# Two stacked self-attention layers: the shift's small operations on GpSimd, and a third native slot in the last stage

## The reference

```python
q = einsum('rc,bcn->brn', Wq, xf) + bq     # 16 rows
k = einsum('rc,bcn->brn', Wk, xf) + bk     # 16 rows
v = einsum('oc,bcn->bon', Wv, xf) + bv     # 128 rows
attn = softmax(einsum('bri,brj->bij', q, k), axis=2)   # 1024 x 1024 per image
out = einsum('bcj,bij->bci', v, attn)
x = gamma * out + x
```

## Time and profile before

| | us |
|---|---|
| median of 3 runs | 213.25 (212.74 to 218.13) |
| the profiled execution | 212.72 |
| its span, first to last instruction | 210.9 |
| PE busy | 187.4 |
| DVE busy | 168.8 |
| ACT busy | 153.3 |
| POOL busy | 149.1 |

### The profile page before, as it was taken

One profiled execution on the slowest core, in us unless ns is written; L12 is line 12 of the kernel. 1 busy time (PEld: TensorE's weight loads), 2 busy tenths in 40 slices (PEclk: granted clock), 3 DMA queues, 4 the chain that ended last, 5 costly groups with the idle time before them and its releaser, 6 DMA issues.

```text
span 210.9 us, 3123 instructions
## 1 busy us (share of the span) xinstructions
PE 187.4 (89%) x1107; PEld 121.6 (58%) x1109; DVE 168.8 (80%) x162; ACT 153.3 (73%) x219; POOL 149.1 (71%) x95
## 2 busy tenths in 40 slices
...
GB/s 166 364 17 177 22 103 2 0 3 3 51 50 2 6 0 99 3 3 0 101 3 3 0 78 26 0 3 53 99 50 0 33 23 50 3 5 14 86 49 51
DMA packets 3871, 9.49 MB, mean 45 GB/s; under 512 B 545, under 2 KB 913, under 8 KB 3857
## 3 DMA queue, kind: packets, MB, share of 16 engines
...
HBM read 2.89 MB, written 2.10 MB: 24 GB/s over the span
## 4 chain that ended last, share of the span: by engine, by line
PE 61%; DVE 21%; ACT 7%; issue 4%; POOL 3%; DMA 2%; SPq 0%; DVEq 0%; POOLq 0%
PE out_psum L692 25%; PE out_psum L690 5%; PE ring L667 5%; PE ring L619 5%; PE ring L643 5%; ACT ring L433 5%; DVE shift_parts L542 5%; PE ring L629 5%; DVE attn_lo L519 5%; DVE shift L539 4%; PE out_psum L693 3%; PE out_psum L726 3%; DVE shift_parts L544 3%; DVE x_all L567 2%; DVE neg_max L524 2%
## 5 line engine op out<-in xcount | busy, mean ns | idle before, releaser
L524 DVE TENSOR_REDUCE neg_max<-ring 128x1 f32<-128x1024 f32 x64 | 76.1, 1220 | 17.5 <-PE ring L645 17.1
L433 ACT ACTIVATE ring<-ring,neg_max 128x1024 f32<-128x1024 f32 x64 | 69.6, 1087 | 19.6 <-DVE neg_max L524 19.5
L346 POOL TENSOR_TENSOR attn_lo<-attn,attn_hi 128x1024 fp32r<-128x1024 f32 x34 | 81.9, 2418 | 2.6 <-ACT attn_hi L451 1.8
L445 ACT ACTIVATE attn<-ring 128x1024 f32<-128x1024 f32 x64 | 63.7, 1025 | 15.5 <-PE ring L669 13.1
L341 POOL TENSOR_SCALAR attn_hi<-attn 128x1024 fp32r<-128x1024 f32 x35 | 39.1, 1124 | 39.8 <-ACT attn L445 36.0
L643 PE MATMUL ring<-qk_swapped,qk 64*128 64x512 f32 x56 | 26.6, 481 | 3.0 <-ACT ring L433 2.4
L669 PE MATMUL ring<-qk_swapped,qk 64*128 64x512 f32 x64 | 28.0, 467 | 0.0
L667 PE MATMUL ring<-qk,qk_swapped 64*128 64x512 f32 x64 | 27.6, 461 | 0.3 <-DVE shift_rows L553 0.2
L645 PE MATMUL ring<-qk,qk_swapped 64*128 64x512 f32 x56 | 27.0, 488 | 0.0
L693 PE MATMUL out_psum<-attn,v 64*128 64x512 f32 x56 | 26.4, 591 | 0.0
L692 PE MATMUL out_psum<-attn,v 64*128 64x512 f32 x56 | 26.4, 591 | 0.0
...
## 6 DMA issues: line engine op xcount, KB each, us to landing
...
qk<-shift_rows SPq DMA_DIRECT2D x7, 8.0 KB
```

The lines of the kernel that those rows point to most:

```text
L346: nc.gpsimd.tensor_tensor(attn_lo[:, k - 1], attn[:, k], attn_hi[:, k - 1].bitcast(fp32), ALU.subtract).then_inc(cut_made["lo", "gpsimd"], 1)
L433: nc.scalar.activation(e[:], e[:], ACT.Exp, bias=neg_max[s][:, i:i + 1], accum_out=row_sum[s][:, i:i + 1]).then_inc(sum_made, 1)
L445: nc.scalar.activation(attn[:, k], ring_tile("ET", s, k)[:].rearrange("p (a n) -> p a n", a=2), ACT.Exp).then_inc(attn_made, 1)
L524: nc.vector.tensor_reduce(neg_max[s][:, i:i + 1], ring_tile("E", s, i)[:], axis=AX.X, op=ALU.max, negate=True).then_inc(max_made, 1)
```

## The change

The three small operations of `parts` move from DVE to POOL: `cut_shift` is removed and `split_shift` does the same on POOL, where the copy is written as a multiplication by 1 plus 0. The parts of the second half of stage 0 lie in columns 8 to 15 of their tile, not in 0 to 7 (`parts_of`). In stage 7 slot 4 becomes native. The five orders are new. Counted over them: DVE has 9 `parts` and 4 `lo` fewer and one `v_lo` more (130 entries become 118); POOL has 9 `parts`, 3 `lo` and one `v_hi` more, one `hi` and one `v_lo` fewer (84 become 95); ACT has one `v_hi` fewer, PE one `PH` fewer. The matmuls of `warm` entries fall from 14 to 12. SP has the same 24 entries.

```diff
-NATIVES = [(0, 1, 4, 7), (0, 7), (0, 7), (0, 7), (0, 7), (0, 7), (0, 7), (0, 7)]
+NATIVES = [(0, 1, 4, 7), (0, 7), (0, 7), (0, 7), (0, 7), (0, 7), (0, 7), (0, 4, 7)]
...
@@ PE_ORDER: begin, around the shifts of stages 0 and 1, and the last stage
-raw.0.0.0 raw.0.1.1 QK.1.0.2 E.0.7.0 E.0.3.1 V.0.0.2 E.0.5.0 E.0.4.1 E.0.0.2 warm.0.4 E.0.2.0 E.0.1.1 E.1.6.2
-warm.0.4 E.0.6.0 warm.0.1 QK.2.0.1 shift.0.0.2 warm.0.3 ET.0.2.2 ET.0.1.0 warm.0.2 E.1.2.2 ET.0.0.1 shift.0.1.0
...
-E.2.5.1 V.1.0.2 ET.0.6.0 shift.1.1.1 PV.0.2 E.2.2.2 ET.0.5.0 QK.3.0.1 E.2.4.0 ET.0.7.2 PV.0.4 ET.1.1.2 PH.0.6
...
-ET.7.2.1 ET.7.5.2 ET.7.6.0 PH.6.3 PH.6.5 PV.6.4 ET.7.4.1 ET.7.7.2 PH.6.6 PV.6.3 PV.6.6 PV.6.5 PV.6.1 ET.7.0.0
-ET.7.1.1 ET.7.3.2 PH.7.6 PH.7.5 PH.7.4 PH.7.2 PV.7.7 PV.7.6 PV.7.5 PV.7.4 PH.7.1 PH.7.3 PV.7.2 PV.7.1 PV.7.3 PV.7.0
+raw.0.0.0 raw.0.1.1 E.0.7.2 E.0.6.0 QK.1.0.1 E.0.2.2 E.0.3.0 E.0.4.1 warm.0.4 E.0.5.2 E.0.1.0 E.0.0.1 warm.0.2
+V.0.0.2 shift.0.1.0 warm.0.1 E.1.3.1 QK.2.0.0 shift.0.0.2 warm.0.3 ET.0.5.2 ET.0.2.1 warm.0.1 ET.0.3.2 E.1.7.0
...
+PV.0.1 E.2.2.2 V.1.0.0 shift.1.1.1 PV.0.3 ET.0.7.2 PV.0.2 E.2.7.1 ET.0.6.0 QK.3.0.2 ET.1.1.0 ET.1.2.1 PH.0.6 PH.0.5
...
+PV.5.7 E.7.3.2 ET.6.7.1 PV.5.6 PV.5.5 V.7.0.0 PH.6.3 PH.6.4 ET.6.2.2 ET.6.5.1 ET.6.0.0 PV.6.7 shift.7.1.1 PV.6.4
+PH.6.6 PH.6.1 PV.6.6 PH.6.5 PV.6.3 ET.7.6.0 ET.7.7.1 ET.7.3.2 PV.6.1 PV.6.5 PV.6.0 PH.6.2 ET.7.5.2 ET.7.1.0 ET.7.4.1
+PV.6.2 PH.7.6 ET.7.2.2 ET.7.0.1 PH.7.5 PV.7.6 PH.7.3 PV.7.7 PV.7.4 PV.7.5 PH.7.1 PH.7.2 PV.7.3 PV.7.1 PV.7.2 PV.7.0
...
@@ POOL_ORDER, whole
-mask.1.0 stack.1.0 v_lo.0.0 hi.0.2 lo.0.2 hi.0.3 lo.0.3 hi.0.6 lo.0.6 hi.0.5 v_lo.1.0 lo.0.5 hi.1.1 lo.1.1 hi.1.2
-lo.1.2 lo.1.3 hi.1.5 hi.1.6 hi.1.4 lo.1.5 hi.2.3 lo.1.6 lo.1.4 hi.2.1 v_lo.2.0 lo.2.3 hi.2.2 lo.2.2 hi.2.4 lo.2.5
-v_hi.3.0 lo.2.4 hi.3.2 hi.2.6 lo.2.6 hi.3.3 v_lo.3.0 lo.3.2 lo.3.3 v_hi.4.0 hi.3.4 lo.3.1 v_lo.4.0 hi.3.6 lo.3.6
-hi.4.2 lo.3.4 lo.4.1 lo.4.2 lo.4.3 hi.4.5 v_hi.5.0 hi.4.4 v_lo.5.0 hi.4.6 lo.4.4 lo.4.6 hi.5.2 hi.5.3 lo.5.3 hi.5.1
-lo.5.1 hi.5.5 lo.5.2 lo.5.5 hi.5.4 hi.5.6 lo.5.4 hi.6.3 v_hi.6.0 v_lo.6.0 hi.6.2 hi.6.4 lo.6.2 v_hi.7.0 lo.6.4
-lo.6.5 v_lo.7.0 hi.7.6 hi.7.4 lo.7.5 hi.7.1 hi.7.3
+mask.1.0 stack.1.0 parts.0.1 parts.0.0 v_lo.0.0 hi.0.2 hi.0.3 hi.0.5 lo.0.3 lo.0.5 parts.1.1 lo.0.2 v_hi.1.0 hi.0.6
+lo.0.6 hi.1.2 hi.1.1 hi.1.3 v_lo.1.0 lo.1.1 lo.1.2 v_hi.2.0 lo.1.3 parts.2.1 hi.1.4 hi.1.6 lo.1.4 hi.1.5 lo.1.6
+lo.1.5 hi.2.1 v_lo.2.0 hi.2.4 parts.3.1 hi.2.3 hi.2.2 lo.2.3 lo.2.2 lo.2.6 v_hi.3.0 lo.2.4 hi.2.5 lo.2.5 v_lo.3.0
+hi.3.2 hi.3.3 parts.4.1 lo.3.3 lo.3.1 lo.3.2 v_hi.4.0 hi.3.4 hi.3.6 lo.3.6 lo.3.4 v_lo.4.0 hi.4.3 lo.4.3 parts.5.1
+hi.4.1 lo.4.1 hi.4.5 v_hi.5.0 v_lo.5.0 lo.4.2 hi.5.3 lo.4.5 lo.4.6 hi.5.1 hi.5.2 parts.6.1 lo.5.2 lo.5.3 lo.5.1
+hi.5.5 hi.5.6 lo.5.4 lo.5.6 hi.6.3 hi.6.4 v_lo.6.0 lo.6.3 hi.6.6 lo.6.1 parts.7.1 lo.6.6 hi.6.2 lo.6.2 v_hi.7.0
+hi.7.6 hi.7.5 lo.7.5 hi.7.1 lo.7.3 lo.7.2
...
@@ SP_ORDER, begin
-swap.1.0 swap.0.0 swap.2.0 place.0.1 place.1.1 swap.3.0 place.2.1 swap.4.0 place.3.1 swap.5.0 place.4.1 swap.6.0
+swap.0.0 swap.1.0 place.0.1 swap.2.0 place.1.1 swap.3.0 place.2.1 swap.4.0 place.3.1 swap.5.0 place.4.1 swap.6.0
...
+            def split_shift(s, h):
+                tiles = tiles_of(s, h)
+                part, count = slice(tiles.start, tiles.stop), len(tiles)
+                if added(s, h):
+                    pool.wait_ge(parts_cleared, 2)
+                    hi, lo = (added_parts[h][:, :, n * count:(n + 1) * count] for n in range(2))
+                    whole = shift[s][:, part][:, None, :].to_broadcast([P, 2, count])
+                else:
+                    hi, lo = (parts_of(s, h)[:, n * count:(n + 1) * count] for n in range(2))
+                    whole = shift[s][:, part]
+                pool.wait_ge(max_made, all_of(nth_max, s, tiles))
+                pool.wait_ge(log_made, nth_log[s, h])
+                nc.gpsimd.tensor_tensor(shift[s][:, part], neg_max[s][:, part], log_sum[s][:, part],
+                                        ALU.subtract).then_inc(shift_made, 1)
+                pool.wait_ge(shift_made, nth_parts[s, h])
+                nc.gpsimd.tensor_scalar(hi, whole, 1.0, 0.0, ALU.mult, ALU.add).then_inc(shift_hi_made, 1)
+                pool.wait_ge(shift_hi_made, nth_parts[s, h])
+                nc.gpsimd.tensor_tensor(lo, whole, hi.bitcast(fp32), ALU.subtract).then_inc(shift_cut, 1)
```

More of the change, by code:

```diff
@@ new lines @@
+V.0.0.2 shift.0.1.0 warm.0.1 E.1.3.1 QK.2.0.0 shift.0.0.2 warm.0.3 ET.0.5.2 ET.0.2.1 warm.0.1 ET.0.3.2 E.1.7.0
+ET.0.0.1 warm.0.1 E.1.5.2 PH.0.2 E.1.4.1 ET.0.1.0 E.1.2.2 PV.0.0 E.1.1.1 ET.0.4.0 E.1.6.2 E.1.0.0 PH.0.3 E.2.0.1
+PV.0.1 E.2.2.2 V.1.0.0 shift.1.1.1 PV.0.3 ET.0.7.2 PV.0.2 E.2.7.1 ET.0.6.0 QK.3.0.2 ET.1.1.0 ET.1.2.1 PH.0.6 PH.0.5
+ET.1.3.0 E.2.6.1 PV.0.5 PV.0.6 E.2.5.2 E.2.4.0 PV.0.4 E.2.3.1 PV.0.7 E.2.1.2 V.2.0.0 ET.1.6.1 ET.1.4.2 PH.1.2
+E.3.5.1 ET.1.0.0 PH.1.3 E.3.6.2 PV.1.2 E.3.1.0 PH.1.1 E.3.3.1 PV.1.0 shift.2.1.2 E.3.7.0 ET.1.5.2 PV.1.3 E.3.0.1
@@ L70 @@
[L70 to L79, removed]
+sum.0.7 sum.0.6 evac.1.0 sum.0.2 sum.0.3 sum.0.4 sum.0.5 sum.0.1 log.0.1 sum.0.0 log.0.0 v_hi.0.0 sum.1.3 attn.0.5
@@ new lines @@
+attn.3.7 attn.3.4 sum.5.1 sum.5.7 sum.5.3 sum.5.0 sum.5.6 sum.5.5 hi.3.5 attn.4.2 attn.4.1 attn.4.0 attn.4.6
+attn.4.3 attn.4.4 sum.5.2 log.5.1 sum.6.4 sum.6.2 attn.4.5 hi.4.6 hi.4.4 sum.6.1 hi.4.2 attn.4.7 sum.6.5 attn.5.3
+attn.5.4 attn.5.1 attn.5.2 attn.5.0 sum.6.0 sum.6.3 sum.6.6 sum.6.7 log.6.1 sum.7.0 attn.5.5 hi.5.4 attn.5.7 sum.7.1
+sum.7.7 attn.5.6 sum.7.6 sum.7.2 attn.6.1 attn.6.3 attn.6.4 v_hi.6.0 attn.6.6 sum.7.4 sum.7.5 sum.7.3 hi.6.1
+attn.6.7 log.7.1 attn.6.5 attn.6.0 attn.6.2 hi.6.5 attn.7.3 attn.7.6 attn.7.7 hi.7.3 attn.7.5 attn.7.4 attn.7.2
@@ L80 @@
+attn.7.1 hi.7.2 attn.7.0
 """
 DVE_ORDER = """
[L82 to L85, removed]
-finish.1.1 parts.3.1 v32.3.0 max.4.7 rows.3.1 max.4.5 lo.2.1 max.4.2 max.4.1 finish.2.0 mask.5.0 stack.5.0 max.4.0
```

76 lines of the change are left out of this document (32 added, 44 removed).

## The result

The changed kernel takes 202.3 us, median of four runs (201.12 to 207.12); the kernel before took 215.69 beside it (212.74 to 218.13). The ratio is 0.948, with a 95% interval of 0.933 to 0.963: faster. (Ratios compare the less disturbed runs of each kernel alone, so they are not the quotients of the medians.) I had said 205.3 us, from 199.5 to 213.5. The profiled run took 201.12 us, 11.6 less than the profiled run of before.

The account below looks back on a forecast made before the run. TensorE, 89% busy, sets the end, partly waiting for the shift's small VectorE instructions, with GpSimd as full in the middle stages; 212.7 − 9.5 − 1.7 + 3.8 + 0 + 0 = 205.3 us, range 199.5 to 213.5.

Parts of the forecast that it names:

- The cause: Shift: each of VectorE's three small instructions waits out GpSimd's running one; 20.2 us together, 13.8 us of TensorE waits.
- The group: Three small shift instructions on GpSimd: 0.28 + 0.16 + 0.28 us and two gaps, about 0.9 us; bounds 0.5 and 3.1.
- −9.5 us of transposition waits: Six TensorE waits at the shift's transposition, 13.8 us in total, shrink by 9.5 us; bounds 0 and −13.8.
- −1.7 us of half clock: Two half-clock stretches after the shifts of stages 0 and 6 hang on TensorE's stands; gain 1.7 us, bounds 0 and −3.4.
- +3.8 us given back by GpSimd: Middle stages: GpSimd ends stage 5 only 6.6 us earlier, so 3.8 us return as TensorE waits for attn_lo.
- my own rule: At stage 5's end, TensorE's 10.4 us lead minus how much earlier GpSimd ends comes back as TensorE waits for attn_lo.
- GpSimd is not the bound: Rival, chance 0.17: TensorE keeps all of 9.5 + 1.7 us, giving 201.5 us, from 198 to 202.5.
- The third native slot, 0: Stage 7: +0.5 us on TensorE against −0.7 to +1 for attn_lo waits; together 0.
- The orders, 0 within 1.5: New engine and DMA-queue orders, with two fewer warm-up matmuls: no effect counted, bounds −1.5 and +1.5 us.
- The signs: Profile after: transposition waits 4 to 5 us, attn_lo waits 3 to 4 us, GpSimd over 95% busy in middle stages.
- signs of being wrong: Group over 1.5 us, GpSimd idling over 1 us a stage before it, or middle stages still at 21 to 25 us.
- the group holds GpSimd's queue: Rival, chance 0.11: GpSimd reaches the group before the logarithm and stands, delaying attn_lo behind it; 217.8 us.

Follow-up runs that it names:

- run 9: Run 8's kernel with the shift's three small operations back on VectorE; 221.18 us.
- run 8: The changed kernel with five more warm-up matmuls on zeros: three ahead of the first energies, two ahead of stage 0's projection of v; 198.18 us.
- run 2: The kernel before, old orders and two native slots in stage 7, with only the three small operations moved to GpSimd; 202.75 us, ratio 0.930 to before.
- run 11: Run 8's kernel plus one unused GpSimd copy of 128 x 768 behind each of the nine groups of small operations; 204.23 us.
- run 6: The changed kernel plus one unused GpSimd copy of 128 x 768 ahead of each of the nine groups of small operations; 208.86 us.
- 7: The changed kernel with slot 4 native in stages 3 and 5 too; 206.81 us.
- 12: Run 8's kernel with v_hi of stages 3, 4 and 5 moved from GpSimd to ScalarE; 199.49 us.
- 3: The changed kernel with slot 4 of stage 7 split again, so two native slots there; 204.09 us, lowest 201.83.
- 4: The kernel before with slot 4 of stage 7 made native and nothing else; 216.05 us, ratio 1.003 to before.
- run 10: Run 8's kernel with slot 4 of stage 7 split again, so two native slots there; 199.38 us.
- 1: The changed kernel, new orders and third native slot, with the three small operations back on VectorE; 225.75 us, ratio 1.026 to before.

## Why the prediction was right, and where it was not

**The cause, right.** Small instructions of VectorE wait out GpSimd's running instruction; on GpSimd one in nine groups is held, behind an attn_lo of VectorE, and the others are not. Four kernels (both orders, both engines) and three timelines show it, with stage 4 of run 9 as the control. The Trainium skill (SBUF — State Buffer, section Who interferes with whom) says that VectorE and GpSimd share a pair of ports, that whoever issues first holds it for a whole instruction, and that a tensor_reduce of VectorE never takes part. The trace agrees on both: 2.02, 2.27 and 2.26 us beside 6.96 us of GpSimd, and a mean of 1220 ns for the row maxima in runs 8 and 9 alike. It binds GpSimd too: its first small instruction takes 1.18 us in stage 7 (170.68 to 171.86), while a VectorE attn_lo runs (to 171.80); the other six average 0.2.

**The group, right.** I had 0.9 us (0.28, 0.16, 0.28 and gaps). It is 0.79 in stage 6, with 0.21 for each: the intercept of the large sizes was 0.07 too high for two inputs and 0.05 too low for one. The rule of the Trainium skill that the prediction cites (GPSIMD Engine Reference, section Engine selection), elementwise work to VectorE, fails for this size beside a busy GpSimd: 0.2 us on GpSimd against 0.17 undisturbed but 0.48 to 1.43 on average on VectorE.

**−9.5 us of transposition waits: too small, −12.9.** I took an average of 1.0 us ahead of the group and did not look for where the new order puts it. In stages 2, 4 and 6 the cut comes 0.94 to 0.97 us after the logarithm. In 3, 5 and 7 it takes 2.3, 2.7 and 4.3, and TensorE has other work then: it waits once, 0.7 us, in stage 7. With the old orders the same move leaves 6.1 us (run 2), so my 4.3 lay between the two.

**−1.7 us of half clock: the tie right, no net gain.** The two stretches that I tied to the late shifts did go, and runs 2 and 9 bear the tie out: four of their five stretches stand at or behind a wait for the transposition. But two came at the start. I had costed the edit there at nothing ("fill waits and cost nothing"); five more warm-up matmuls at that place are worth 3.2 us (run 8). Whether the two fewer, or the new order of the start, brought the half clock was not tried.

**+3.8 us given back by GpSimd: the step that failed.** I dated the end of the kernel by GpSimd's end of stage 5, at 156.9 us. GpSimd's load up to there is as summed (109.3 us for my 108.8), its idle time 5.2 us for my 2.3, and it ends at 160.2, only 3.3 us earlier than before. By my own rule 10.4 − 3.3 = 7.1 us would then have come back, and the time would be 208.6 us; yet the kernel ends 11.6 us earlier. What lies behind that point shrank from 47.4 to 39.1 us. I had counted GpSimd's idle time up to 163.55 us alone. Right behind it, before, GpSimd stood 6.50 us:

```profile
170.05 1.05 POOL L341 TENSOR_SCALAR attn_hi<-attn 128x1024 fp32r<-128x1024 f32 x1 [6.50 <-ACT attn L445]
```

After, it goes on at once:

```profile
155.51 4.72 POOL L350 TENSOR_TENSOR attn_lo<-attn,attn_hi 128x1024 fp32r<-128x1024 f32 x2
160.20 3.03 POOL L345 TENSOR_SCALAR attn_hi<-attn 128x1024 fp32r<-128x1024 f32 x2
```

GpSimd's end of a stage is not TensorE's: the products that need attn_lo stand late enough in TensorE's order, and TensorE waits 0.3 us for it in all, not 3 to 4. The load itself was rightly feared. It is at 97% in the middle stages, and each further microsecond on it costs 0.67 (5.0 of 7.5, run 11) to 0.68 (5.8 of 8.5, run 6). The rival "GpSimd is not the bound" gave 201.5 us, and its band of 198 to 202.5 holds the median of 202.3, which is just under my forecast's own band (202.5 to 208.5). Its argument, that much of GpSimd's work has slack to the product that uses it, is what the traces show; its title is not, as added load costs time. That TensorE and GpSimd are both at the bound stays argued: the two runs that took load off GpSimd (7, 12) gained nothing, each by a new or longer wait.

**The third native slot, 0: right** (runs 3, 4; 0.9 us in run 10). **The orders, 0 within 1.5: too narrow, and right in time by luck.** In span x clock they give 3 us with the move (run 2 against after) and lose 2 to 3 without it (runs 1, 9); the half clock at the start takes the gain back. I weighed them entry by entry; what the traces show of their effect is that the group of stage 6 stands right behind its logarithm.

Against the profiled run, for which the sum was made, 205.3 is 4.2 us too high: 3.4 from the waits (−12.9, not −9.5), 2.3 from what came back (+1.5, not +3.8), 0.2 from the work, less 1.7 for the gain by the clock that did not come. The errors partly cancel, and the range of 199.5 to 213.5 was wide.

**The signs.** GpSimd over 95% busy in the middle stages came true (97%). The waits of 4 to 5 us at the transposition are 0.9, and the new waits for attn_lo of 3 to 4 are 0.3. Of the signs of being wrong none showed but once: the group takes 0.79 us in stage 6 and 1.77 in stage 7 alone, where its first instruction is held. In stages 2 to 6 GpSimd idles 1.5 us in all in front of the group, so the rival "the group holds GpSimd's queue" didn't come. From the logarithm of stage 2 to that of stage 6 a stage takes 19.7 us on average, where it was 23.4.

**Open.** Run 9 waits 12.5 us for the transposition, less than the 13.8 of before, and still has 2 to 4 us more in span x clock. The other idle time grew from 9.7 to 14.1 us (219.8 − 193.2 − 12.5), in waits for ScalarE (3.6 us at L671); which order entry makes them wasn't tried. Why the clock at the start differs between executions of one kernel is not shown by any run.
